# A cleared tile for TensorE's warm-up, and two steps moved in a fused attention and feed-forward layer

## The reference

```python
x = x + attn(layernorm(x), qkv, o_proj, gamma, beta)     # has a norm and a residual of its own
x = x + ffn(layernorm(x), gate_w, up_w, down_w, scales)  # weights rounded to fp8, I = 768
x = x + s4d(layernorm(x), D, log_dt, A, C)               # along the axis of length 2
x = x + ffn(layernorm(x), gate_w, up_w, down_w, scales)
# attn: q, k, v = norm(x) @ qkv; softmax(q k^T / 16, causal) @ v @ o_proj + x
# ffn:  (silu(x @ gate * gs) * (x @ up * us)) @ down * ds
```

## Time and profile before

| what | value |
|---|---|
| median of 3 runs | 122.87 us (122.67, 122.87, 123.37) |
| the profiled execution | 123.42 us |
| its span, from the first to the last instruction | 121.6 us |
| TensorE busy | 115.3 us (95%), 685 entries |
| VectorE busy | 98.2 us (81%) |
| GpSimd busy | 83.8 us (69%) |
| ScalarE busy | 77.4 us (64%) |
| share of TensorE in the chain that ended last | 69% |

### The profile page before, as it was taken

How to read it: one execution, slowest core, us unless ns; L and a number is a source line. 1 busy time by engine, 2 the same in 40 slices (tenths; PEclk the granted TensorE clock), 3 DMA queues, 4 the chain that set the end, 5 groups by cost and what they waited for, 6 DMA issues and landing times.

```text
span 121.6 us, 2132 instructions
## 1 busy us (share of the span) xinstructions
PE 115.3 (95%) x685; PEld 79.9 (66%) x685; DVE 98.2 (81%) x231; ACT 77.4 (64%) x147; POOL 83.8 (69%) x163
## 2 busy tenths in 40 slices
PE   5999999999999998999999999999999999999960
PEld 5798889467678666644678545577445589756650
DVE  0458999996998996969797898999899985797482
ACT  0452599968465368858938269785489665589700
POOL 2205599999999878997943588689976782037731
PEclk9999999999999999999999999999999999999996
DMA  3989920000000000000000000000000000000505
GB/s 98 363 244 411 356 59 0 0 0 0 0 0 3 0 8 0 0 0 0 0 0 5 0 0 0 0 3 5 0 0 0 3 0 5 0 0 0 172 0 172
DMA packets 5614, 5.80 MB, mean 48 GB/s; under 512 B 1618, under 2 KB 4836, under 8 KB 5604
## 3 DMA queue, kind: packets, MB, share of 16 engines
q1 hardware_dynamic: 4632, 5.53, 13.2%
q10 hardware_dynamic: 972, 0.15, 0.7%
HBM read 4.63 MB, written 1.05 MB: 47 GB/s over the span
## 4 chain that ended last, share of the span: by engine, by line
PE 69%; DVE 12%; ACT 5%; POOL 5%; DMA 4%; issue 3%; SPq 0%; POOLq 0%; DVEq 0%
PE psum L1326 18%; PE psum L1360 11%; PE psum L1265 8%; PE psum L1240 7%; PE psum L1202 6%; DMA qkv_sb<-in_qkv 4%; PE psum L1195 3%; PE psum L1340 3%; PE psum L1188 3%; PE psum L1158 3%; DVE stats L749 2%; ACT h_rows L583 2%; PE psum L1287 2%; DVE x_plus L1018 2%; PE psum L1151 2%
## 5 line engine op out<-in xcount | busy, mean ns | idle before, releaser
L637 ACT ACTIVATE gated<-psum,scales 128x512 f32<-128x512 f32 x24 | 16.3, 680 | 12.2 <-PE psum L1326 9.9
L1360 PE MATMUL psum<-down,f_head 128*128 128x256 bf16 x96 | 22.0, 273 | 0.0
L1360 PE MATMUL psum<-down,f_tail 128*128 128x256 bf16 x96 | 22.0, 273 | 0.0
L1049 DVE SCALAR_TENSOR_TENSOR fused<-psum,up_scales_fit,gated 128x512 f32<-128x512 f32 (+1 forms) x25 | 17.8, 716 | 3.2 <-PE psum L1326 1.9
L447 POOL TENSOR_TENSOR f_tail<-fused,f_head 128x512 f16<-128x512 f32 x10 | 11.8, 1182 | 10.5 <-ACT f_head L643 9.2
L643 ACT ACTIVATE f_head<-fused 128x512 f16<-128x512 f32 (+1 forms) x25 | 15.2, 608 | 2.6 <-DVE fused L1049 2.3
L295 POOL TENSOR_TENSOR rstd<-var_eps,neg_half 128x2 f32<-128x2 f32 (+1 forms) x15 | 11.7, 777 | 2.2
L1057 DVE TENSOR_TENSOR f_tail<-fused,f_head 128x512 f16<-128x512 f32 (+1 forms) x15 | 10.1, 676 | 3.8 <-ACT f_head L643 3.7
L1326 PE MATMUL psum<-h_head,up 128*128 128x512 f16 x44 | 13.1, 379 | 0.0
L1326 PE MATMUL psum<-h_head,gate 128*128 128x512 f16 x44 | 13.1, 379 | 0.0
L1326 PE MATMUL psum<-h_tail,gate 128*128 128x512 f16 x44 | 13.1, 379 | 0.0
(11 more groups left out here) (183 smaller groups left out, 271.7 us busy)
## 6 DMA issues: line engine op xcount, KB each, us to landing
x_in<-in_x SPq DMA_DIRECT2D x4, 256.0 KB, 5.8
qkv_sb<-in_qkv SPq DMA_DIRECT2D x1, 768.0 KB, 4.4
gate_raw<-in_gate_w SPq DMA_DIRECT2D x1, 768.0 KB, 7.7
up_raw<-in_up_w SPq DMA_DIRECT2D x1, 768.0 KB, 9.2
down_raw<-in_down_w SPq DMA_DIRECT2D x1, 768.0 KB, 10.9
out<-x_in SPq DMA_DIRECT2D x3, 256.0 KB, 2.1
wo_sb<-in_o_proj SPq DMA_DIRECT2D x1, 256.0 KB, 5.5
down_scale_all<-in_down_scale SPq DMA_DIRECT2D x1, 128.0 KB, 6.0
```

Of the source, the lines that this page charges most:

```text
L637: act.activation(gated[:, m % 2, :], psum[:, BANK_GATE[m % 2], :], ACT.Silu, scale=gate_scales[:, m:m + 1]).then_inc(gated_ready, 1)
L1049: dve.scalar_tensor_tensor(out=fused[:, m % FUSED, cols], in0=psum[:, BANK_UP[m % 2], cols], scalar=up_scales_fit[:, m:m + 1], in1=gated[: ...
L1360: last = pe.matmul(down_columns(n, t), part[:, m, t * P:t * P + P], down16[:, m, :], start=(m == 0 and (t % 2 == 0 or n == 2 * B - 1) and ...
```

## The change

`warm_up` calls matmul in place of transpose, on a new tile `warm` that VectorE clears in its first instruction, 20 times in place of 17. It now stands ahead of the wait for the identity and waits for the cleared tile. On GpSimd the root for tiles 2 and 3 of the second norm changes places with taps_begin. On VectorE row_max(0) and row_max(1) move behind g_second_half and xn_second.

```diff
--- before.py
+++ after.py
@@ -32,7 +32,7 @@
 P = 128
 EPS = 1e-5
 MASKED = -3.0e38
-WARM_UP = 17
+WARM_UP = 20
 ROUND = 1.5 * 2.0**23
 FP8_LARGEST = 464.0
 LOG2E = float(np.float32(np.log2(np.e)))
@@ -99,6 +99,7 @@
         beyond = sb("beyond", [P, 4])
         down_scale_all = sb("down_scale_all", [P, H])
         ident = sb("ident", [P, P])
+        warm = sb("warm", [P, P])
         ident16 = sb("ident16", [P, P], BF16)
         ones = sb("ones", [P, P])
         ones16 = sb("ones16", [P, 2], BF16)
@@ -149,6 +150,7 @@
         down_scale_loaded = sem("down_scale_loaded")
         taps_spread, taps_loaded, out_stored = sem("taps_spread"), sem("taps_loaded"), sem("out_stored")
         pool_step = sem("pool_step")
+        warm_ready = sem("warm_ready")
         ident_ready, consts_ready = sem("ident_ready"), sem("consts_ready")
         params_turned, params_ready = sem("params_turned"), sem("params_ready")
         scales_turned, scales_ready = sem("scales_turned"), sem("scales_ready")
@@ -428,8 +430,8 @@
             angle_squares()
             round_weight(1, up16, gate_up_ready)
             inverse_std(1, 0, 2, negative_mean=True)
+            inverse_std(1, 2, 2, negative_mean=True)
             taps_begin()
-            inverse_std(1, 2, 2, negative_mean=True)
             pool.wait_ge(bound_squared, 1)
             pool.tensor_tensor(bound[:, 4, :], bound[:, 3, :], pos_half[:], ALU.pow).then_inc(bound_ready, 1)
             inverse_std(1, T, 2, negative_mean=True)
@@ -939,6 +941,7 @@
                 dve.wait_ge(x1_ready, k + 1)
                 tile_stats(1, [k], x1)
 
+            dve.memset(warm[:], 0.0).then_inc(warm_ready, 1)
             first_stats(0)
             normalise((0, 1))
             copy_k()
@@ -955,10 +958,10 @@
             reduce_angle()
             grid_begin(0)
             grid_end(0)
+            g_second_half()
+            xn_second()
             row_max(0)
             row_max(1)
-            g_second_half()
-            xn_second()
             grid_begin(1)
             v_half(0)
             grid_end(1)
@@ -1136,13 +1139,14 @@
                 return psum[:, bank, start:start + width]
 
 
+            def warm_up(times):
+
+                for n in range(times):
+                    pe.matmul(column(BANK_NORMS, 0, P), warm[:], warm[:], start=True, stop=True)
+
+            pe.wait_ge(warm_ready, 1)
+            warm_up(WARM_UP)
             pe.wait_ge(ident_ready, 1)
-            def warm_up(times):
-
-                for n in range(times):
-                    pe.transpose(column(BANK_NORMS, 0, P), ident[:], ident[:])
-
-            warm_up(WARM_UP)
 
             def turn_w(w):
                 pe.wait_ge(qkv_loaded, 16)
```

More of the change, by code:

```diff
@@ L1136, in column @@
                 return psum[:, bank, start:start + width]
-            pe.wait_ge(ident_ready, 1)
             def warm_up(times):
                 for n in range(times):
-                    pe.transpose(column(BANK_NORMS, 0, P), ident[:], ident[:])
+                    pe.matmul(column(BANK_NORMS, 0, P), warm[:], warm[:], start=True, stop=True)
+            pe.wait_ge(warm_ready, 1)
             warm_up(WARM_UP)
+            pe.wait_ge(ident_ready, 1)
             def turn_w(w):
```

## The result

The changed kernel takes 125.35 us (median of 6 runs, 124.19 to 126.09) against 122.82 for the kernel before (6 runs, 122.67 to 123.37). The ratio is 1.0168 with an interval of 1.013 to 1.0206, which is 1.6 to 2.5 us slower. The ratio is taken without the slowest run of the changed kernel, 126.09 us; the median of the other five is 125.15. Forecast were 124.5 and 123.5 to 125.3: the direction and the place are right, and the size is short. The median of all six lies 0.05 us above the range, that of the five inside it.

A forecast was written before the change was run, and what follows sets the result against it. The prediction took qkv's transfer, then TensorE working without a hole, to bound the front. The profiled 123.42 us + 1.2 for the warm-up - 0.1 for GpSimd's order gave 124.5, range 123.5 to 125.3.

The forecast's parts named there:

- An ordinary f32 product is two passes: Warm-up on TensorE: 20 products are 40 passes, each as long as a transpose at the same clock.
- The warm-up outlasts the wait for qkv and nothing absorbs it: Front of the kernel: qkv's transposes end 1.23 us later, and the whole 1.2 passes to the end.
- The start: Warm-up on TensorE: begins at 0.98 us behind VectorE's memset, 0.53 us sooner than before.
- The length: Warm-up on TensorE: 40 passes end at 7.58 us, which delays qkv's transposes; the term is +1.2 us.
- The typical rise of 4.45 us: TensorE's clock goes from 1.2 to 2.4 GHz typically 4.45 us after its first entry.
- Time outside the span: Whole execution: 1.8 us around the span of 121.6, kept in the forecast sum.
- GpSimd's order: Inverting tiles 2 and 3 ahead of the taps: -0.08 us, ends 0 and -0.40; the copy of probs is late next.
- the risk that I had put at 0.2 us: GpSimd waiting for late statistics ahead of the taps and the bound's power, for which VectorE waits: at most +0.2 us.
- VectorE's order: Two row maxima behind g and xn on VectorE: worth 0, ends -0.1 and +0.1 us.
- That products bring the clock sooner: Rival 1, warm-up: ordinary products raise the clock sooner; 123.5 us or less chance 0.08, of which 0.03 below 122.87.
- That a cleared product is one pass: Rival 2, warm-up: a product of the cleared tile is one pass, hidden before qkv; 122.8 us, chance 0.04.
- Absorption near 48 us: Rival 3: the delay is absorbed in part where 0.40 us of GpSimd's lateness vanish; 124.2 us, chance 0.10.

The follow-up runs named there:

- forty transposes: The changed kernel with 40 transposes of the identity in place of 20 products, against the kernel before: 125.18 us, ratio 1.0176.
- bf16: The changed kernel with 42 products of a cleared tile in bf16 in place of 20 in f32, against the kernel before: 123.6 us, ratio 1.0044.
- the warm-up alone: The new warm-up with GpSimd's and VectorE's lists in the old order, against the kernel before: 125.15 us, ratio 1.015.
- the thirty products: The changed kernel with 30 products in place of 20, against the kernel before: 127.15 us, ratio 1.0335.

## Why the prediction was right, and where it was short

- **An ordinary f32 product is two passes.** Right: 20 calls, 40 entries, and 40 transposes do the same. Where I stated it from spread_taps and fold, it held for a cleared tile too.
- **The warm-up outlasts the wait for qkv and nothing absorbs it.** Right: the delay of 1.52 us at the parameters' transpose is in the span as 1.5.
- **The start.** TensorE began at 1.04 where I had 0.98, because VectorE's memset began at 0.82 and not at 0.72 (it was 0.17 long and not 0.20).
- **The length: this term was too small.** The forecast span was 121.6 + 1.2 - 0.1 = 122.7; the median span of the six runs is 123.1. These 0.4 us are one half of the 0.85 by which the time was short. In the profiled execution I had the transposes at 7.58, and they came at 7.88. 0.06 us are the start, 0.16 the first space (the second entry came 0.37 us after the first), and 0.08 what a later rise, 4.8 us after the first entry where I had taken 4.45, leaves once my spacings of 0.217 and 0.11 are put right to 0.213 and 0.112. The 0.217 had a longer first space in it.
- **The typical rise of 4.45 us was the mis-sized value.** I had read it from the median of the old kernel's runs. But a rise anywhere before qkv's transposes leaves the old kernel at one time: 11 of its 23 runs on the second occasion lie between 122.76 and 122.95 us. While it waits for qkv the old kernel hides the rise, so its median says little about the typical moment. The changed kernel has no such wait and pays 0.1 us for every slow pass more; its spans spread from 122.3 to 123.6 us, where 20 of those 23 lie between 121.0 and 121.9. Worked out from the spacing, the rises in the nine profiles with a warm-up lie 3.8 to 5.9 us after the first entry, the middle one 5.4. With 5.4 the same sum gives a delay of 1.7 and a span of 123.2.
- **Time outside the span: held constant without a reason.** I had 1.8 us for it. In two of the six runs of the changed kernel 2.9 to 3.0 us lie outside the span, in the other four 1.9 to 2.1. That makes up the other half of the 0.85. One of the two is the profiled execution (125.97 - 123.1). The forty transposes (1.9 to 2.3) and bf16 (1.9 to 2.9) show it too; in the other experiments and in the kernel before it is 1.75 to 1.9 in every run. Its cause is open. So the changed kernel's time is 2.5 us over the old one's, but what the warm-up makes of it is nearer the 2.1 of the warm-up alone.
- **GpSimd's order.** Right in its result (-0.08 forecast, -0.04 at the first product of gate, nothing at the end) and in what is late next, the copy of probs. But I wrote that the power for the bound "comes behind both in either order" and gave it no delay but the risk. It came 2.04 us later (49.00 against 46.96), 0.5 more than the front's delay: GpSimd stood 0.12 us for the statistics of tile 3, 0.27 for issue ahead of the taps, and a pair of small products ran 1.10 us where it ran 0.52, while the root's own power ran only 0.71 where it ran 1.23. VectorE's wait for it grew from 0.95 to 1.55. This is the risk that I had put at 0.2 us. It stayed hidden because the tails of h had 0.5 us of slack: VectorE had them ready at 50.41 before, and TensorE took them at 50.92. Now it is 52.36 and 52.42, and the slack is gone.
- **VectorE's order.** Right: worth nothing. The maxima end at 22.95, the table load on ScalarE runs from 23.73.
- **The rivals.** That products bring the clock sooner fell with the rises: 3.8 to 5.9 us after the first entry in the five profiles with f32 products, 4.3 to 5.5 in the three with transposes alone, where the rival needed 2.1 or less. That a cleared product is one pass fell with the 40 entries; its price was also wrong, as 0.53 us of an earlier rise are 2.4 slow spaces and 0.26 us, not 5 and 0.5. Absorption near 48 us fell with the thirty products.

## What to carry to other kernels

Count a warm-up in passes and in time, never in calls: here an f32 transpose was one pass and an f32 product two, and qkv's transposes, though their operand had landed near 5.6 us, began behind the last pass at 7.88. Every pass beyond the arrival of the first operand was paid: 20 more passes cost 2.0 to 2.2 us in the spans, 0.11 each at full clock. A pass ahead of the rise takes 0.21, but if the rise stays where it is, it moves another pass from 0.21 to 0.11, so by this estimate it costs 0.11 as well. Compare the end of the warm-up with the landing of the transfer behind it, in the trace. The chain of waits alone does not tell: with eleven products the transfer is gone from it too, and nothing was lost. And when a wait on the critical engine goes, ask first which neighbour is ready next: 0.40 us at this one turned into 0.04.

## What the runs showed of the hardware that I had not expected

- Transposes alone brought the full clock: 40 of them, in f32, had a mean spacing of 0.176 us, with 12 at 272 ns behind them. The Trainium skill, page "TensorE: Matmul & The Clock Gate", section "Part 4: PE-mode transpose", says beside its figures for bf16 that the full clock doesn't engage for transposes. The f32 transposes of these runs disagree, and the runs decide; no run here has transposes in bf16.
- Starting TensorE 0.47 us sooner bought nothing that can be measured: 123.25 and 123.01 us with 10 and 11 products against 123.08 and 123.05. In the ten profiles the clock rose between 3.4 and 5.9 us after the first entry, whatever the entries were. What sets it within that spread these runs don't show.
- The weight loads of an ordinary f32 product took 333 ns each at the low clock, those of a transpose 231 (226 before), and yet the entries of both kinds stood 0.213 us apart.
